# Moving the softmax exponential of an audio-tower kernel from the table block to the end of the slot before, with Exp's table kept until the refine gelus

## The reference

```python
scores = einsum('bsqd,bskd->bsqk', x, x) / sqrt(D);  h = softmax(scores) @ x   # inside a tile
h = h + attn(layernorm(h))        # bind, decaying scan over the sequence, unbind
h = h + ffn(layernorm(h))
# ffn: router (gelu layer, 8 logits, top 2 of 8, softmax of the two), then twice:
#   ctrl = gelu(ctx @ w1) @ w2    for a shared unit and for the two chosen experts
#   v_next = sigmoid(a) * v - softplus(b) * (x - mu);  x_next = x + 0.1 * sigmoid(g) * v_next
#   mixed by the router's weights, moved by halt = sigmoid(gelu(x @ hw1) @ hw2)
# and at the end  out = x + iw * (gelu(x @ rw1) @ rw2)     ("refine")
```

## Time and profile before

| what | value |
|---|---|
| median of 3 runs | 774.84 us (774.31 to 776.21) |
| the profiled execution, its own time | 774.78 us |
| its span, first to last instruction | 773.0 us |
| PE busy | 728.1 us, 94% |
| DVE busy | 610.8 us, 79% |
| ACT busy | 569.3 us, 74% |
| POOL busy | 372.1 us, 48% |
| mean granted TensorE clock | 0.974 |

### The profile page before, as it was taken

One profiled execution on the slowest core, in us unless ns is written; L12 is line 12 of the kernel. 1 busy time (PEld: TensorE's weight loads), 2 busy tenths in 40 slices (PEclk: granted clock), 3 DMA queues, 4 the chain that ended last, 5 costly groups with the idle time before them and its releaser, 6 DMA issues.

```text
span 773.0 us, 14304 instructions
## 1 busy us (share of the span) xinstructions
PE 728.1 (94%) x4516; PEld 615.8 (80%) x4516; DVE 610.8 (79%) x1430; ACT 569.3 (74%) x1359; POOL 372.1 (48%) x438
## 2 busy tenths in 40 slices
PE   5757999999999999999999999999999999999986
PEld 3646778888888888888888888888888888888875
DVE  4847778978978878878878878879789789789662
ACT  4665778787787787887887886887887887877663
POOL 1426446445555555545545555454564564463310
PEclk9688999999999999999999999999999999999997
DMA  8300000000000000000000000000000000000000
GB/s 326 123 15 1 8 0 12 10 21 3 19 22 2 21 21 3 20 22 0 22 22 1 22 22 1 21 22 1 22 21 1 8 8 2 8 8 1 8 8 14
DMA packets 11611, 17.27 MB, mean 22 GB/s; under 512 B 1232, under 2 KB 10504, under 8 KB 11024
## 3 DMA queue, kind: packets, MB, share of 16 engines
q1 hardware_dynamic: 11536, 16.35, 6.2%
HBM read 13.20 MB, written 3.15 MB: 21 GB/s over the span
## 4 chain that ended last, share of the span: by engine, by line
PE 66%; ACT 15%; DVE 12%; issue 5%; POOL 1%; DMA 1%; SPq 0%; POOLq 0%; ACTq 0%; DVEq 0%
PE ctl L495 23%; PE ctl L511 10%; PE ctl L472 5%; PE ctl L501 4%; PE ctl L514 4%; ACT L906 4%; ACT L1060 3%; DVE both L1324 3%; DVE work L1319 3%; PE cd L472 3%; PE cd L666 3%; PE ctl L481 3%; ACT work L909 2%; DVE both L1325 2%; PE ctl L482 2%
## 5 line engine op out<-in xcount | busy, mean ns | idle before, releaser
L375 POOL TENSOR_TENSOR hm_lo<-gl,mexp 128x256 fp32r<-128x256 f32 x144 | 127.8, 913 | 124.2 <-DVE gl L1256 120.7
L495 PE MATMUL ctl<-w2e_hi,hm_hi 128*128 128x512 f32 (+1 forms) x432 | 160.9, 382 | 0.1
L495 PE MATMUL ctl<-w2e_lo,hm_hi 128*128 128x512 f32 (+1 forms) x432 | 150.3, 360 | 0.0
L965 ACT ACTIVATE work<-ctl 128x256 f32<-128x256 f32 (+1 forms) x144 | 70.2, 487 | 68.6 <-PE ctl L514 59.1
L1242 DVE TENSOR_TENSOR hm_hi<-ge,mexp 128x256 fp32r<-128x256 f32 x144 | 88.7, 631 | 20.0 <-ACT ge L946 17.7
L495 PEld LDWEIGHTS ctl<-w2e_hi,hm_hi 128*128 128x128 f32 x432 | 82.1, 190 | 24.7 <-DVE hm_hi L1242 8.0
L511 PE MATMUL ctl<-w2e_hi,hm_lo 128*128 128x512 f32 (+1 forms) x432 | 100.0, 357 | 0.0
L495 PEld LDWEIGHTS ctl<-w2e_lo,hm_hi 128*128 128x128 f32 x432 | 82.3, 191 | 10.5
L511 PEld LDWEIGHTS ctl<-w2e_hi,hm_lo 128*128 128x128 f32 x432 | 74.6, 188 | 13.6 <-POOL hm_lo L375 0.2
L381 POOL TENSOR_TENSOR rg_lo<-rg,rg_hi 128x512 fp32r<-128x512 f32 x23 | 37.7, 1639 | 70.8 <-ACT rg_hi L902 70.8
L967 ACT ACTIVATE work<-ctl 128x256 f32<-128x256 f32 x144 | 54.5, 378 | 0.0
(11 more groups left out here) (211 smaller groups left out, 2040.3 us busy)
## 6 DMA issues: line engine op xcount, KB each, us to landing
work<-params_dram SPq DMA_DIRECT2D x3, 1152.0 KB, 13.2
xT<-turned_dram SPq DMA_DIRECT2D x24, 128.0 KB, 2.2
out_dram<-y SPq DMA_DIRECT2D x24, 128.0 KB, 1.7
xa<-x_dram SPq DMA_DIRECT2D x16, 128.0 KB, 2.2
par<-params_dram SPq DMA_DIRECT2D x1, 1280.0 KB, 10.9
work<-params_dram SPq DMA_DIRECT2D x2, 512.0 KB, 11.2
xa<-x_dram SPq DMA_DIRECT2D x8, 119.0 KB
par<-params_dram SPq DMA_DIRECT2D x1, 512.0 KB, 16.0
```

Of the source, the lines that this page charges most:

```text
L375: TT(hm[1][:, j, c, :], gl[:, c, part, :], pairs(tile, j, c), ALU.mult).then_inc(done, 1)
L495: mm(dst[:, a:z], hm[0][:, j, c, :], w2e[i][:, c, a:z], start=(c == 0 and i == 0), stop=False)
L965: AF(tan[tile.s][:, 1:kinds, j, :], ctl_t[:, D:kinds * D].rearrange("p (a d) -> p a d", a=kinds - 1), ACT.Tanh, scale=0.5)
```

## The change

Three things are moved in ACT's program. The exponential of a tile now stands in the slot in which the tile is z, between `tw` and `unit(n, 1)`, with the load of its table inside `softmaxed`. The load of the gelus' table stands once more, in front of `refine_units`, so tanh and copies between the two run under Exp's table. The table block loses its Exp part. `rates()`, two small exponentials of the start, goes with the first exponential.

```diff
@@ softmaxed
             def softmaxed(e):
 
+                nc.scalar.preload_act_table_set("exp_and_others")
                 passed(act, smax_v, e)
                 passed(act, eT_ps, e, back=1)
@@ slot, its beginning
-                if e.exists() and not t.exists():
-                    softmaxed(e)
-                    if e.low == 0:
-                        rates()
-
                 if f.exists() and f.low == 0:
                     table_of_gelus()
                     constants()
@@ behind unit(t, 1)
+                if t.exists() and e.exists():
+                    table_of_gelus()
 
                 if o.exists():
@@ the table block
                 if t.exists():
-                    if e.exists():
-                        nc.scalar.preload_act_table_set("exp_and_others")
-                        softmaxed(e)
                     softplus_of(m, t)
                     table_of_gelus()
@@ behind tw, ahead of unit(n, 1)
+                if z.exists():
+                    softmaxed(z)
+                    if z.low == 0:
+                        rates()
 
                 if n.exists():
                     unit(n, 1, u2_sb, u2_ps, ctl[0], 3)
```

## The result

The changed kernel takes 765.8 us in the median of four runs (763.96 to 767.29) against 774.58 (772.3 to 776.21): a ratio of 0.9888, 95% interval 0.9853 to 0.9922. Its profiled execution took 766.59 us with a span (first to last instruction) of 764.8, against 774.78 and 773.0: 8.2 us less on both counts. The forecast was 766.5.

What follows compares the result with a forecast made beforehand. PE was taken to bound the kernel. Slots 2 to 21 at 0.38 us (7.6), slot 1 (0.14) and the start (0.5) took 8.2 us off the profiled 774.78: 766.5 us, own range 764.5 to 769, full range 763 to 773.

Steps and rivals of the forecast that it cites:

- What bounds the kernel: Whole kernel: PE bounds it, busy 582.6 of 590 us; taking work from ACT gains only where PE waits.
- The first part, 0.26 us at L481: At PE's wait for sab before L481: sab comes, and L481 starts, 0.26 us earlier in a slot.
- POOL's interference: At DVE's products: it takes 1.34 us instead of 0.99, since POOL's u0 and vu run through all of it.
- Rival 2: The wait at L481 vanishes without POOL's interference: 0.56 us a slot, 763.3 us; chance 0.06.
- PE's readiness: Before L481: PE is ready at 402.84, ahead of L481's new start at 402.91, so 0.26 us stands narrowly.
- L481's wait is under 0.1 us: Sign at L481 that the forecast is right: PE's wait there falls below 0.1 us.
- The second part, 0.14 us before L495: At PE's wait for mask_hi: from L481 to the second L495 1.04 us instead of 1.18, 0.14 gained.
- The slot's end: Behind tw: moved load and exponential make unit(n, 1) 0.29 us late, hidden by idle times; cost nothing.
- The second load of the gelus' table: Ahead of the refine gelus: they start 0.25 us late; cost taken as 0.02 us a slot, from 0 to 0.25.
- Rival 1: At L472: the router product pays for the gelu load in full, 3.6 us gained, 771.1 us; chance 0.14.
- rival 4: Ahead of the refine gelus: the load costs extra time; slower from 0.53 us extra, 792 us at 1.28; chance 0.11.
- The start: Slots -1 and 0: 1.25 us lost ahead of w2a, 1.81 us back in slot 0; net 0.5 us gained.

Runs made afterwards that it cites:

- the copy: The changed kernel with one more copy of 128 x 256 on ACT at the head of the table block: 767.59 us.
- the run with 1.29 us: The changed kernel with a load of Exp's table, but no exponential, at the head of the table block: 772.76 us.
- the POOL move: The changed kernel with POOL's subtractions vu and u0 moved behind its masks hm_lo of iteration 2: 763.53 us.
- The added load: The changed kernel with a load of Softplus's table ahead of every load of Exp's, behind tw: 781.91 us.
- The six other traces named above: Traces with ACT's start order as in the changed kernel; from the router's gelu of slot -1 to that of slot 0, 24.55 to 24.90 us.
- c0: The changed kernel measured again, nothing altered: 764.63 us in six runs, ratio 0.9857 to the kernel before.

## Why the prediction held, step by step

**What bounds the kernel.** Right. The period fell by 0.38 us where ACT's part of the chain was 1.81. A reader of the chain alone would have forecast 20 times 1.81, 36 us.

**The first part, 0.26 us at L481.** Right in size. The block's first 0.53 us of length are free (the copy, and the block without its load), and by the 0.46 us wait of the run with 1.29 us the limit is near 0.83; behind it the slot follows at about half. Slot 22 as a model for the rest was what carried the number: from the end of `output` to the end of `sab` the changed kernel takes 397.68 - 393.81 = 3.87 us, 3.88 there.

**POOL's interference.** That it costs DVE time is shown by the POOL move, for the two sums: 1.11 us each beside u0 and vu, 0.69 without. The reason that I gave was not right: in the kernel before, `products` lasts 0.99 us from 399.95, and POOL's `vu` runs beside nearly all of it:

```profile
400.07 1.45 POOL L425 TENSOR_TENSOR vu<-x,par 128x256 f32<-128x256 f32 x1
```

What counts is which one is already running. An operation of DVE that starts while one of POOL runs is longer by what POOL's still needs, less 0.13 to 0.18 us: the two sums of the changed kernel, with 0.56 us of POOL's operation left, by 0.42; `products` by 0.34 with 0.52 left, by 0.50 with 0.68 left (the block load), and by nothing with 0.17 left (the kernel before). One of POOL that starts behind DVE's takes up to 1.45 us instead of 0.73. The profile's spans on POOL are rough, so these are estimates. The Trainium skill's page "SBUF — State Buffer", section "SBUF: two separate sides", has DVE operations with two SBUF inputs and reading GpSimd operations share a pair of ports that one of them holds for its whole instruction; these durations agree with that, and no run here shows the lock itself. Rival 2, a gain without it, had 0.54 us a slot with the second load paid; with u0 and vu away the slot has 29.52 - 28.98 = 0.54. So the price of that rival was right, and it needed a change of its own to come true. My account of PE's readiness was off: I put it at 0.44 us behind L742, and it is 0.36. "0.26 stands, narrowly" was too cautious: 0.15 us of waiting were left. By this measure the sign "L481's wait is under 0.1 us" did not come, though the profile marks no wait there.

**The second part, 0.14 us before L495.** Right: 1.04 us from L481 to the second L495.

**The slot's end.** Right that it is free. I had `unit(n, 1)` 0.29 us late and 0.36 us of idle time left; 0.52 is left, so it was 0.13 late. The next activation starts 0.09 us before the accumulator read ends, which my 1.81 us, measured to a load, had not seen; that is 0.09 of the 0.16 us. The added load cost 0.69 us, near the 0.77 that I had from the idle time before `unit(n, 2)`, but that agreement is luck. The way there is another: it was `mexp` that PE waited for, over DVE's `hm_hi`, and its room, 1.29 - 0.69 = 0.60 us, happens to be like the 0.52 that I took.

**The second load of the gelus' table.** I took 0.02 us within 0 to 0.25; it is 0.04 (without the load, and with the copy behind `xj_hi`). The hand-over is 0.11 us here, from `xj_hi`'s end at 388.34 to the weight load for L472:

```profile
388.45 0.41 PEld L472 LDWEIGHTS cd<-xfT,par 128*64 128x64 f32 x4 [0.41 <-ACT xfT L922]
```

That is between my two ends and near the one I took. Rival 1 is refuted, but narrowly: the room was used up by the first load, and the next 1.29 us were paid in full. This is also where rival 4 would have come from. Its slope was right: I forecast a slower kernel from 0.53 us of extra load time, and 1.29 us made 794.7 us, where I had written 792. (A slot pays 30.43 - 29.52 = 0.91 us, as that rival had it; two slots of that run took 1.4 and 1.7 us more than the others.)

The Trainium skill's page "ScalarE: Activation LUTs", section "What ACT_TABLE_LOAD costs", adds 1380 ns of drain to the load. No run here shows it: two loads side by side take 1.29 us each, and of the changed kernel's 99 loads 94 are followed by the next instruction within 0.03 us, and the other five by one that waits for PE or DVE. Its rule in "Table sets: the hidden batching unit", to batch by set, would have advised against this change; here the fourth load of a slot costs 0.04 us since it stands in idle time.

**The start and the rest.** Here the sum came out right with terms that did not. Between the router's gelus of slots -1, 0 and 1 the changed kernel takes 23.30 and 25.51 us against 22.34 and 27.99: 0.96 us lost and 2.48 gained, so in this pair of profiles the start brought 1.5 us and not 0.5. It is a figure of the pair and not of the change. The six other traces named above take 24.55 to 24.90 us for the first stretch, so in them the move ahead of `w2a` cost 2.2 us or more. L481 starts 13.06 us behind the gelu of slot -1 in the kernel before, 13.76 in the changed one and 14.43 in its repeat c0: 0.70 and 1.37 us late, where I had 1.25. The rest comes behind L481, where PE ran at a lower clock for longer. The windows from 16 us behind that gelu on, of the kernel before and of c0, in the columns of the earlier trace rows; the third number from the right is the granted clock:

```profile
36.75:40.75 4.00, 4.00 (x17) 2.94 (x16) 2.90 (x8) 1.22 (x5) 1.14 (x3) 0.95 0.00 0
38.42:42.42 4.00, 4.00 (x12) 3.19 (x11) 1.55 (x4) 1.01 (x5) 0.25 (x1) 0.56 0.00 0
```

I had no term for that. Slot 0 is settled by its own windows, of the kernel before, of the run with the gelus' load twice (which is the changed kernel again) and of the changed kernel:

```profile
43.09:71.08 27.99, 16.87 (x74) 12.60 (x75) 18.34 (x42) 14.47 (x34) 12.82 (x14) 0.76 0.04 10
44.47:70.65 26.18, 16.85 (x74) 12.50 (x75) 18.80 (x42) 15.63 (x35) 13.54 (x14) 0.74 0.03 10
44.91:70.42 25.51, 16.05 (x74) 11.98 (x75) 18.79 (x42) 15.62 (x35) 13.53 (x14) 0.80 0.04 11
```

Where the same 74 matmuls keep PE as busy as before, at about the same clock, the slot is 1.81 us shorter: my 1.81. The other 0.67 us, between two executions that are alike in this slot, go with the clock, 0.80 instead of 0.74. Over both stretches the kernel before takes 50.33 us, the changed one 48.81 and the six other traces 50.05 to 51.07, so the start brings anything from 1.5 us gained to 0.7 us lost, at granted clocks that differ between the executions; no run holds the clock fixed. My net 0.5 lies within that, but 1.25 for the first term was too little in most of them.

Slot 1 brought 0.32 us instead of 0.14, slots 2 to 21 together 8.1 instead of 7.6, of which slot 2 alone 0.72. With the start that makes 9.9 us in this profile, and 8.6 in c0's. The profiled execution shows 8.2, because 1.7 us were lost at the two ends, where nothing was changed. So the steady slots carried the forecast, and that the whole came out within 1 us of it is in part luck. At the start it is one product that shows it, before and after in the chain that ended last:

```profile
14.48 1.15 PE cd L666 x4
```

```profile
14.38 2.09 PE cd L666 x4
```

The same four matmuls took 0.94 us longer, and the granted clock from 14 to 16 us is 1.00 in both, so the rows do not say why. At the end the load at L906 of slot 23 stood at 744.04 and stands at 734.97, 9.07 us earlier; from there the kernel before needed 29.0 us and the changed one 29.8. The windows over the last microseconds, before and after, in the same columns:

```profile
769.00:773.00 4.00, 1.20 (x8) 1.00 (x8) 0.85 (x2) 0.04 (x1) 0.00 (x0) 1.00 0.10 35
```

```profile
759.00:764.80 5.80, 3.04 (x12) 2.71 (x12) 1.27 (x3) 0.93 (x4) 0.00 (x0) 0.50 0.07 24
```

TensorE was granted 1.0 of its speed, 2.4 GHz, at the end of the one execution and 0.5, 1.2 GHz, at the end of the other, after stretches in which it waited a good deal in both. The lower clock is not foreign to the kernel before (0.50 there from 762 to 766 us), and the changed kernel's profile c0 has 1.00 over its last 6 us. In the 14 traces of all kernels here the stretch from the router's gelu of slot 22 to the end takes 80.8 to 84.2 us, the shortest at a mean clock of 0.98 and the longest at 0.89. So this is not of the change. The medians (8.8 us less, and 12.3 in the comparison with c0) do not decide between 8.2 and 9.9; their intervals are some 5 us wide.

## What to carry to other kernels

An engine's time on the chain that ended last is an upper bound. Ask how far behind the next engine is if that time vanishes, and the one after it; here 1.81 us shrank to 0.97 at DVE, to 0.26 at its end, and PE took 0.38 in all. Where some iteration of the trace already lacks the part that is to be removed, read the new schedule from it, contention included. A table load has no fixed price: the same 1.28 us cost 0.04 us a slot where it fits a wait, 1.29 as a second one in the same place, and 0.69 at the slot's end, and idle time between two hand-overs of the same chain isn't room.

## What the runs showed that I had not expected

- Of two equal table loads placed side by side only one was in the trace (49 of 71 asked for). The two Exp loads of slots -3 and -2, with other work between them, were both there (24 of 24).
- A sum of DVE over 512 columns takes 0.69 us alone and 1.11 when one of POOL's subtractions is running as it starts; `products` over 768 columns takes 0.99 to 1.49 by the same rule, and POOL's own of 256 columns 0.73 and up to 1.45.
- The two ends of this kernel do not repeat. The router's gelu of slot -1 comes at 19.7 to 22.4 us in the 14 traces and the stretch behind that of slot 22 varies by 3.4 us, while slots 2 to 21 take 582.51 us in the changed kernel's one profile and 582.61 in the other, at a clock of 1.00. A term for a start of some 50 us cannot be read from one pair of profiles.
